# A layer of attention and routed experts: setup for the first batch alone, the rest dealt over two units, and filler products counted per step

## The reference

```python
xn = layernorm(x)
q, k, v = split(xn @ w_qkv)                       # 16 heads of 8
wei = softmax(where(causal, q @ k.T * 8 ** -0.5, -inf))
attn = (wei @ v) @ w_proj + b_proj
top2, idx = top_k(xn @ Wg.T, 2);  w = softmax(top2)
y = sum over k of w[k] * (gelu(xn @ W1[idx[k]] + b1[idx[k]]) @ W2[idx[k]] + b2[idx[k]])
out = x + attn + y
```

## Time and profile before

| | us |
|---|---|
| median of 3 runs | 864.74 (863.75 to 866.88) |
| profiled execution | 862.67 |
| its span, first to last instruction | 860.9 |
| PE busy, share of span | 737.2 (86%) |
| DVE busy | 557.6 (65%) |
| ACT busy | 449.3 (52%) |
| POOL busy | 282.8 (33%) |
| mean granted clock of TensorE | 0.849 |

### The profile page before, as it was taken

One profiled execution on the slowest core, in us unless ns is written; L12 is line 12 of the kernel. 1 busy time (PEld: TensorE's weight loads), 2 busy tenths in 40 slices (PEclk: granted clock), 3 DMA queues, 4 the chain that ended last, 5 costly groups with the idle time before them and its releaser, 6 DMA issues.

```text
span 860.9 us, 15136 instructions
## 1 busy us (share of the span) xinstructions
PE 737.2 (86%) x5021; PEld 418.5 (49%) x5021; DVE 557.6 (65%) x2164; ACT 449.3 (52%) x717; POOL 282.8 (33%) x454
## 2 busy tenths in 40 slices
PE   3683788988888989879999999889999999999995
PEld 2562344434445545545555455546455555546543
DVE  5649455556575676757676766757767667676656
ACT  2212133243445666656655665646666665566663
POOL 7103835657121323323231313122332223131421
PEclk9555566559786999999898989889999989897998
DMA  6997301203074342606134342505242423430074
GB/s 156 174 148 247 133 25 35 77 32 79 18 221 137 83 124 58 173 13 166 59 92 113 87 120 81 151 13 146 80 126 87 120 84 88 137 109 4 22 180 124
DMA packets 96261, 88.74 MB, mean 103 GB/s; under 512 B 8368, under 2 KB 83672, under 8 KB 96184
## 3 DMA queue, kind: packets, MB, share of 16 engines
q1 hardware_dynamic: 91432, 78.05, 35.2%
q0 software_dynamic: 4544, 9.35, 3.3%
q10 hardware_dynamic: 208, 0.38, 0.2%
...
## 4 chain that ended last, share of the span: by engine, by line
PE 66%; DVE 18%; SPq 4%; DMA 3%; issue 3%; ACT 3%; POOL 2%; another core or an unknown queue 0%; ACTq 0%; DVEq 0%
PE ov L780 19%; PE aux L748 16%; PE aux L838 10%; PE aux L790 6%; DVE maxes L970 5%; DVE junk L971 3%; SPq L449 3%; PE sc L702 3%; PE aux L795 3%; DMA hid<-in_L_ffn_W 2%; PE sc L703 2%; PE sc L704 2%; DVE maxes L966 2%; DVE xrow L1024 2%; PE aux L818 1%
## 5 line engine op out<-in xcount | busy, mean ns | idle before, releaser
L655 ACT ACTIVATE probs<-sc 128x1024 f32<-128x1024 f32 (+3 forms) x384 | 295.1, 810 | 252.6 <-PE sc L766 235.0
L748 PE MATMUL aux<-kT,qT 32*128 32x512 f32 (+3 forms) x768 | 244.3, 484 | 67.4 <-DVE maxes L971 19.5
L568 POOL TENSOR_SCALAR_AFFINE_SELECT probs<-probs 128x256 f32<-128x256 f32 x256 | 103.9, 409 | 390.3 <-ACT probs L655 386.0
L970 DVE TENSOR_REDUCE maxes<-aux 128x1 f32<-128x128 f32 (+2 forms) x384 | 161.1, 420 | 66.5 <-PE aux L748 65.5
L966 DVE TENSOR_REDUCE maxes<-aux 128x1 f32<-128x512 f32 x256 | 163.4, 684 | 60.9 <-PE aux L748 52.4
L748 PEld LDWEIGHTS aux<-kT,qT 32*128 32x128 f32 x768 | 108.2, 205 | 181.7 <-DVE maxes L971 50.4
L780 PE MATMUL ov<-probs,v 128*32 128x512 f32 (+3 forms) x1536 | 186.8, 562 | 3.6 <-POOL probs L568 3.4
L766 PE MATMUL sc<-qT,kT 32*128 32x512 f32 (+3 forms) x768 | 170.8, 466 | 5.5 <-DMA qT<-mT 5.1
L971 DVE CUSTOM_DVE_ANT_0 junk<-aux,cst 128x128 f32<-128x128 f32 x512 | 140.6, 283 | 17.5 <-PE aux L748 16.3
L593 POOL DMA_INDIRECT ys<-ysb,back x78 | 76.0, 974 | 77.4 <-issue 46.2
L838 PEld LDWEIGHTS aux<-w2b,hid 128*128 128x128 f32 x624 | 78.7, 197 | 41.8 <-DVE maxes L971 28.8
...
## 6 DMA issues: line engine op xcount, KB each, us to landing
...
```

The lines of the kernel that those rows point to most:

```text
L568: nc.gpsimd.affine_select(out=block_, in_=block_, compare_op=ALU.is_ge, fill=0.0, base=0, pattern=[[0, 2], [1, P]], channel_multiplier=-1) ...
L655: nc.scalar.activation(probs[:, s % 2, 2 * half:2 * half + 2, 0:cols], pair(part)[:, :, 0:cols], ACT.Exp).then_inc(sc_done, 1)
L748: nc.tensor.matmul(bank(part)[:, 0:cols], qT[n % 3][rows, P * i:P * i + P], kT[n % 3][rows, k0:k0 + cols], start=True, stop=True).then_inc ...
L970: nc.vector.reduce_max(maxes[:, i, other, h:h + 1], bank(part)[:, 0:cols - P], axis=AX.X)
```

## The change

The setup handles batch 0 alone. Stats and norm of batches 1 and 2 are started in it, with the norm of batches 1 to 3 now on GpSimd; all three vg groups of batch 0 stand in it (the groups are regrouped by batch, 12 in all); 24 maxima instead of 16 come ahead of unit 0, with 20 fillers before them and three before each pair. The table `BESIDE` deals the rest over the steps of unit 0 (xt, vg, stats and norm of batch 3, the split of W1 in two parts, cast and store, and the clearing in 13 pieces) and of unit 1 (the routing in 12 pieces, `route`, of one to six instructions each). The routing's scratch moves from `probs` to the space of `w2b`, `attnT` and `xsin`, and the first exponential no longer waits for the routing. Relay 0 is issued by SP and ScalarE, three transfers each. W1 is loaded by eight transfers. The transfers that zero the fourth rows of the queries fall away for the first three units, which a memset has zeroed.

The 64 scatters go to 22 steps, from step 10 of unit 1 to step 7 of unit 3. The experts' blocks are dealt over units 4 to 14, eleven instead of twelve, three or four a unit (five units with three, six with four). The stream of maxima is dealt anew: a unit takes its own last 16 in its first steps (24 in units 0 and 2) and then the next unit's first 32 (24 in unit 1); the last unit, which had none, has 16. `rows` comes one step after its `negate`. Loading for the first expert group starts in step 8 instead of 7.

A filler is now a product of 128 x 128 x 384 of type f32r, in one record instead of two per product. `fill` counts how many a step gets: each part's columns, times passes, times its share of the array, are summed from the step's start to the next step or to the next hidden product, and what lacks to 4000 (units 0 to 3), 2900 (expert units) or 3300 (unit 15) is filled up. Applied to the list this gives 339 products: 56 in the setup, 23, 37, 50 and 44 in units 0 to 3, 8 or 9 in each of units 4 to 13 (six in step 0, none in step 1, up to one in step 9, two in step 11), 14 in unit 14 and 30 in unit 15. In units 0 to 3 a full step has one to four, steps with short values up to eight.

```diff
+FILL = 384
...
+EARLY_M = 24
+
+FFN_UNIT = list(range(4, UNITS - 1))
 GROUP_OF = {u: f for f, u in enumerate(FFN_UNIT)}
 NGRP = len(FFN_UNIT)
 FIRST = [NBLK * f // NGRP for f in range(NGRP + 1)]
-VG_TILES = [list(range(t, min(t + 3, NT))) for t in range(0, NT, 3)]
+VG_TILES = [[TPB * b + t for t in x] for b in range(B) for x in ((0, 1, 2), (3, 4, 5), (6, 7))]
+PIECES = 13
...
-    parts = [("weights",), ("stats", 0), ("stats", 1), ("norm", 0), ("xt", 0), ("xt", 1)]
+    parts = [("weights",), ("stats", 0), ("norm", 0), ("xt", 0), ("xt", 1)]
     parts += [("qk", 0, j, c) for c in range(2) for j in range(2)]
-    parts += [("relay", n) for n in range(2)] + [("clear",), ("fetch",), ("relay", 2)]
-    parts += [("norm", 1), ("xt", 2), ("stats", 2), ("xt", 3), ("vg", 0), ("norm", 2), ("stats", 3), ("xt", 4), ("vg", 1),
-              ("xt", 5), ("vg", 2), ("norm", 3), ("xt", 6), ("vg", 3), ("xt", 7)]
-    maxima = [("max", 0, m) for m in range(HALF_M)]
-    for r in range(4, len(VG_TILES)):
-        parts += maxima[2 * r - 8:2 * r - 6] + [("vg", r)]
-    parts += [("top_two",)] + maxima[14:] + [("negate", 0, 0), ("prefix",), ("rows", 0, 0), ("slots",)]
-    parts += [("w1", e) for e in range(E)] + [("scatter", t, 0) for t in range(4)]
+    parts += [("fetch", e) for e in range(E)] + [("relay", 0), ("relay", 1)]
+    parts += [("vg", 0), ("stats", 1), ("norm", 1), ("vg", 1), ("vg", 2), ("stats", 2), ("norm", 2)]
+    parts.append(("warm", -1, 0, 20))
+    for i in range(0, EARLY_M, 2):
+        parts += [("warm", -1, i + 1, 3)] + with_negations(maxima()[i:i + 2])
+        if i + 2 == HALF_M:
+            parts.append(("rows", 0, 0))
     return parts
+BESIDE = {
+    (0, 0): [("relay", 2), ("w1", 0), ("clear", 0), ("clear", 1)],
+    (0, 1): [("xt", 2), ("w1", 1), ("clear", 2)],
+    (0, 2): [("xt", 3), ("w1", 2), ("w1_out", 0), ("clear", 3)],
+    (0, 3): [("vg", 3), ("w1", 3), ("w1_out", 1), ("clear", 4)],
+    (0, 4): [("vg", 4), ("stats", 3), ("norm", 3), ("w1_out", 2), ("clear", 5)],
+    (0, 5): [("vg", 5), ("xt", 4), ("w1_out", 3), ("clear", 6)],
+    (0, 6): [("xt", 5), ("vg", 6), ("clear", 7)],
+    (0, 7): [("vg", 7), ("w1", 4), ("clear", 8)],
+    (0, 8): [("vg", 8), ("xt", 6), ("w1", 5), ("clear", 9)],
+    (0, 9): [("xt", 7), ("vg", 9), ("w1", 6), ("w1_out", 4), ("clear", 10)],
+    (0, 10): [("vg", 10), ("w1", 7), ("w1_out", 5), ("clear", 11)],
+    (0, 11): [("vg", 11), ("w1_out", 6), ("clear", 12)],
+    (1, 0): [("route", 0), ("w1_out", 7)],
+    (1, 1): [("route", 1), ("route", 2)],
+    (1, 2): [("route", 3)],
+    (1, 3): [("route", 4), ("gate",), ("prefix",)],
+    (1, 4): [("route", 5)],
+    (1, 5): [("route", 6)],
+    (1, 6): [("route", 7)],
+    (1, 7): [("route", 8)],
+    (1, 8): [("route", 9), ("route", 10)],
+    (1, 9): [("route", 11)],
+}
...
-def unit_parts(n):
+def counts(n):
+    if n in GROUP_OF:
+        return [3] * NS
+    first = {0: [8, 8, 8], 1: [6, 5, 5], 2: [8, 8, 8]}.get(n, [6, 5, 5])
+    rest = {0: 32, 1: 24, UNITS - 1: 0}.get(n, 32)
+    return first + [rest * (i + 1) // 9 - rest * i // 9 for i in range(9)]
+def unit_parts(n, stream):
...
-    full_array = ("rows_in", "turn", "columns", "project", "qk", "down", "hidden")
     step_of = (2, 3, 4, 5, 7, 8) if len(subs) == 6 else range(2, 2 + len(subs))
-    here = 0
     for s in range(NS):
-        count = -(-len(todo) // (NS - s))
-        if n == 0:
-            count = 8 if s < 4 else 6
-        group = take(count)
-        if not any(x[0] in full_array for x in parts[here:]):
-            parts.append(("warm", n, s))
-        here = len(parts)
-        parts.extend(row_phase(n, s, group[:4]))
-        parts.extend(group[4:] + after_maxima(group))
+        due, late_rows[:] = list(late_rows), []
+        group = take(counts(n)[s])
+        parts.append(("step", n, s))
+        only = [x for x in group if x[0] == "max"]
+        parts.extend(row_phase(n, s, only[:4]))
+        parts.extend(x for x in group if x not in only[:4])
         if s == 0 and f is None:
             late_values()
         if s > 0:
             parts.append(("values", n, s - 1))
-        if s == 0 and n > 0:
-            parts.append(("rows", n, 1))
-        if s == 3 and n == 0:
-            parts.append(("rows", 0, 1))
-        if s == 7 and n + 1 < UNITS:
-            parts.append(("rows", n + 1, 0))
+        parts.extend(due)
+        parts.extend(BESIDE.get((n, s), []))
...
-        if n < 2:
-            i = 4 + 30 * n + (5 * s + 1) // 2
-            for x in range(i, 4 + 30 * n + (5 * s + 6) // 2):
-                parts.append(("scatter", x, 0))
+        step = NS * n + s - (NS + 10)
+        if 0 <= step < 22:
+            parts.extend([("scatter", 0, 0)] * (TOPK * NT * (step + 1) // 22 - TOPK * NT * step // 22))
...
+def aim(n):
+    return 2900 if n in GROUP_OF else 3300 if n == UNITS - 1 else 4000
+def array_use(part):
+    what = part[0]
+    if what == "scores":
+        return SUB[part[2]][3] // 2
+    if what == "values":
+        return 4 * SUB[part[2]][3]
+    if what == "max":
+        return MAXES[part[2] // HG][2] // 4
+    return {"turn": 1024, "xt": 1024, "columns": 1024, "rows_in": 1024, "project": 2048, "down": 2048, "rows": 256,
+            "qk": 3 * W, "vg": 9 * (C + E), "hidden": 12 * BK}.get(what, 0)
+def fill(parts):
+    out = []
+    for i, x in enumerate(parts):
+        if x[0] != "step":
+            out.append(x)
+            continue
+        end = next((j for j in range(i + 1, len(parts)) if parts[j][0] == "step" or parts[j][0] == "hidden"), len(parts))
+        n, s = x[1:]
+        short = aim(n) - sum(array_use(y) for y in parts[i:end])
+        if short > 0:
+            out.append(("warm", n, s, -(-short // FILL)))
+    return out
...
-        tmp = probs[:, :, :, :].rearrange("p a b w -> p (a b w)")
+        tmp = w2all[:, :, :, :].rearrange("p a b c -> p (a b c)")
+        scan = [attnT[:, 416 * i:416 * i + 416].rearrange("p (t e) -> p t e", e=E) for i in range(2)]
+        tmp2 = xsin[:, :, :].rearrange("p t c -> p (t c)")
...
+                        if n == 0:
+                            continue
                         sp.dma_start(qT[i][r:P:4, :].bitcast(F32), (kqh, kqh, kql)[r][rows, 1, :].bitcast(F32)) \
                             .then_inc(relayed[i], 16)
-                    sp.dma_start(qT[i][3:P:4, :].bitcast(F32), mid(zero[0:32, :], T // P)).then_inc(relayed[i], 16)
+                    if n >= 3:
+                        sp.dma_start(qT[i][3:P:4, :].bitcast(F32), mid(zero[0:32, :], T // P)).then_inc(relayed[i], 16)
                 elif what == "fetch":
-                    sp.dma_start(w1_in, W1.rearrange("e h i -> h e i")).then_inc(w1_loaded, 16)
+                    e = part[1]
+                    sp.dma_start(w1_in[:, e, :], W1[e]).then_inc(w1_loaded, 16)
                 elif what == "clear":
+                    i = part[1]
                     sp.wait_ge(dest_set, 2)
-                    tiles = xs.rearrange("(g v p) c -> v p g c", p=P, v=SPARE)
-                    for i in range(SPARE):
-                        sp.dma_start(tiles[i], mid(zrow[:, i, :], SLOTS // P // SPARE)).then_inc(xs_zero, 16)
+                    sp.dma_start(xs.rearrange("(g v p) c -> g p v c", p=P, v=SPARE)[i], zrow).then_inc(xs_zero, 16)
                 elif what == "rows":
                     n, c = part[1:]
                     sp.wait_ge(aux_a, A_AFTER[part])
                     sp.dma_start(qT[n % 3][3:P:4, W * c:W * c + W].bitcast(F32), mT[:, :].bitcast(F32)) \
                         .then_inc(rows_set[c], 16)
-                elif what == "w1":
+                elif what == "w1_out":
...
-                    if i == 1:
+                    if i == 0:
...
+                elif what == "norm" and part[1] > 0:
+                    i = part[1]
+                    pool.wait_ge(rstd_ready, i + 1)
+                    for t in range(TPB * i, TPB * i + TPB):
+                        last_ = nc.gpsimd.tensor_scalar(xn[:, t, :], xn[:, t, :], meanvar[:, t, 0:1], rstd[:, t:t + 1],
+                                                        ALU.subtract, ALU.mult)
+                        if t % 4 == 3:
+                            last_.then_inc(xn_ready, 1)
...
+                if part == ("relay", 0):
+                    act.wait_ge(zeroed, 9)
+                    act.wait_ge(aux_d, D_AFTER["qk", 0, 1, 1])
+                    for r in range(3):
+                        act.dma_start(qT[0][r:P:4, :].bitcast(F32), (kqh, kqh, kql)[r][0:32, 1, :].bitcast(F32)) \
+                            .then_inc(relayed[0], 16)
...
-                    if (n, s) == (0, 0):
-                        act.wait_ge(slots_ready, 1)
...
-                        for _ in range(WARM):
-                            nc.tensor.matmul(bank(unit)[:, 0:P], ident, upper, start=True, stop=True)
+                        for _ in range(part[3]):
```

(8 more changed lines are left out.)

146 lines of the change are left out of this document (71 added, 75 removed).

## The result

The changed kernel takes 856.1 us (median of 19 runs, 848.9 to 863.7) against 863.3 for the kernel before in the same comparison (19 runs): ratio 0.991, 95% interval 0.989 to 0.993. So the change is a gain of 7 us, not of 75. The profiled execution took 850.3 us with a span of 848.6.

What follows compares the result with a forecast made beforehand. It took the start as bound by a chain, later stretches by TensorE, busy 84 to 91% and slower at low clock. Start and units 0 to 3 243.5 + expert units 502 + last 40 = 786 us span, 3.8 over it: 790; range 766 to 830.

Steps and rivals of the forecast that it cites:

- First exponential 41.5: Start: first maximum at 27.5, maxima 9.5, negation to exponential 4.5, so first exponential at 41.5 us; bounds 38 and 50.
- Unit 0, 51: Unit 0: three steps of 5.5, nine at 3.4 and smaller terms make 51 us, before 76.8; bounds 45 and 65.
- unit 1, 50: Unit 1: VectorE's maxima, low halves, turns and routing sum to 44, with waits 50 us; bounds 44 and 56.
- Units 2 and 3, 101: Units 2 and 3: GpSimd's scatter steps 84, four more steps 13.6, late loads 3, making 101 us; bounds 94 and 120.
- 3.4 would be TensorE's pace: Scatter steps of units 2 and 3: TensorE alone would need 3.4 us a step, less than GpSimd's 4.35 or 3.7.
- Eleven expert units 502: Units 4 to 14: 517 less 25 saved by fillers, plus 4.5 for blocks and 5.5 for maxima; bounds 490 and 517.
- Last unit 40: Unit 15: 39 us before, +4 for 16 maxima coming in, -3 for shorter fillers, making 40 us.
- (1): Rival, 13%: the low clock stays in units 0 to 3, 24 steps take 5 us; time 831 us.
- (2): Rival, 15%: maxima wait for the relay behind W1's loads, or unit 4 for its loads; 12 to 15 us, time 804.
- (3): Rival, 9%: expert units' step 0 fillers come on the path and the clock falls all the same; time 826 us.
- (4): Rival, 3%: f32r fillers do not hold TensorE's clock, expert units run at 1.2 GHz; time some 1000 us.
- The rule on GpSimd: Unit 1's routing: two-input VectorE instructions share ports with GpSimd and meet only selects; some 3 us, inside the unit's bounds.

Runs made afterwards that it cites:

- experiment 1: Changed kernel with GpSimd's memsets of qT, mneg and v waiting for VectorE's normalisation of the first batch; ratio 0.979 to the kernel before.
- experiment 14: Kernel of experiment 9 with 16 instead of 24 maxima in the setup, the rest dealt to unit 0's first three steps; ratio 0.971 to the kernel before.
- Experiment 15: Kernel of experiment 9 with at least six fillers in steps 1 and 2 of units 0 to 3; ratio 0.974 to the kernel before.
- experiment 9: Kernel of experiment 1 with 16 maxima moved from unit 15 to units 2 and 3, last row transposed in the next unit's step 0; ratio 0.966 to the kernel before.
- experiment 10: Kernel of experiment 1 with the 64 scatters dealt over the same 22 steps by step length; ratio 0.974 to the kernel before.
- experiment 2: Changed kernel with the 64 scatters replaced by plain SyncE transfers of the same bytes, output wrong; ratio 0.977 to the kernel before.
- experiment 6: Changed kernel without the six fillers in step 0 of the eleven expert units; ratio 1.006 to the kernel before.
- 7: Kernel of experiment 1 with fewer fillers in the start and none in step 0 of unit 0; ratio 0.981 to the kernel before.
- 11: Kernel of experiment 1 with the six fillers of each expert unit's step 0 moved to that step's end; ratio 0.979 to the kernel before.
- 12: Kernel of experiment 1 with scatters dealt by step length and expert units' step 0 fillers moved to that step's end; ratio 0.971 to the kernel before.
- experiment 13: Kernel of experiment 9 with the scatters dealt by the length of the step; ratio 0.965 to the kernel before.

## Why the prediction was wrong

It had the mechanisms mostly right and called the sign, but all six terms of the sum were too low. Errors of one sign don't cancel, and the range was made as if they did.

- **"First exponential 41.5"**, 57.6 measured. The start's old chain is gone as forecast. Two parts failed. The memsets moved with the first batch were not among the moved instructions that I costed; experiment 1 prices them at 7 us. And "from the negation to the exponential that needs it takes 4.4 us" forgot the eight further maxima and their fillers, which the list puts between the two; experiment 14 prices them at 7.6. The rest, some 1 to 2 us, lies ahead of the first maximum, which came at 28.75 in experiment 1 where 27.5 was forecast.
- **Unit 0, 51; unit 1, 50**: 55.6 and 53.1. "5.5 a step" for the first three was the term: steps 1 and 2 of unit 0 take 7.7 and 8.7. I took VectorE's part as the step's length. (The norm on GpSimd was also mis-sized, 0.78 us a piece where 0.35 were assumed, but no select waited for it.) The trace of the changed kernel shows the two engines in turn, in step 1 of unit 2:

```profile
170.85 2.48 DVE L1060 TENSOR_REDUCE maxes<-aux 128x1 f32<-128x512 f32 x4 [0.50 <-issue]
171.60 3.01 PE L836 MATMUL aux<-kT,qT 32*128 32x512 f32 x5 [0.40 <-issue]
174.54 1.94 PE L868 MATMUL ov<-probs,v 128*32 128x512 f32 x8
176.41 1.12 PE L883 MATMUL aux<-cst,ot 128*128 128x128 f32 x4
177.17 1.63 PE L878 MATMUL aux<-wh 128*128 128x384 f32 x4
```

  With three banks TensorE can't run ahead of VectorE by more than three maxima, so values, turn and fillers come behind the maxima, at 1.2 GHz, while VectorE has nothing (it idles 2.06 us there before its next reciprocal). Experiment 15 shows that feeding TensorE more doesn't shorten these steps, though the clock over the first three steps is higher than in 9 in three of the four units. That the order of the parts would, or more banks, is argued and not tested.
- **Units 2 and 3, 101**: 112.2. GpSimd as the new bound was right, and its sum too: 84 us were forecast for the twenty scatter steps of units 2 and 3, by the same prices 92 for all 22, and 92.0 is what it takes where it is hardly ever idle (experiment 10). What failed is the other engine's price and with it the overlap: "3.4 would be TensorE's pace", and without scatters these 22 steps take 85 us, not 75 (experiment 2: 6.8 in unit 1, 48.7 in unit 2 and 29.6 in unit 3). Of two sums so near each other the larger is not the length, because the deal is even and the steps are not: in those of 2 us three scatters are late, in those of 8.7 they leave GpSimd idle (11.6 us in the changed kernel), and what is late at step 7 of unit 3 makes the steps behind it late (step 8 takes 8.4 us instead of the 4.9 of experiment 2). The loss against experiment 2 is 17 us in units 2 and 3, part of it through the low clock after a wait; but 2 to 6 us of it belong to this one execution, since the four traces with the same list there (experiments 1, 6, 7 and 11) take 106.6 to 109.9. The new deal brings the two units down to 101.6 (experiments 10 and 12), so it accounts for about half of the loss.
- **"Eleven expert units 502"**: 521. The saving was right: steps 0 to 2 take 8.74 us on average instead of 10.96, 2.2 a unit against the 2.3 forecast, though the clock still fell in four units. So was the price of the longer maxima between the blocks: from the first hidden product of unit 7 to its first scores it takes 9.81 us without fillers (experiment 6) and took 9.23 before, 0.6 against 0.5. Wrong was that the six fillers stand "where TensorE waits for VectorE anyway": they stand behind such a wait, and the same stretch of unit 7 takes 10.96 us with them and 9.81 without: 1.15 us a unit, 13 in all. Unit 4 pays 5.9 more than unit 7 in its hidden phase, at the low clock, after TensorE waited 3.95 us for the first blocks' W1 (3 were forecast, in the stage before); in experiment 1, where that wait is 1.2, it pays 1.9. Their loads stand on SP behind the packed rows (issued at 265.92) and x:

```profile
266.34 4.82 SPq L539 DMA_DIRECT2D xrow<-in_L_attn_x  x4
272.26 2.78 SPq L559 DMA_DIRECT2D w1b<-w_scr  x3
277.90 0.55 PE L790 MATMUL sc<-xsh,w1b 128*128 128x256 f32 x1 [3.95 <-issue]
278.25 0.41 PE L791 MATMUL sc<-xsl,w1b 128*128 128x256 f32 x1
```

- **"Last unit 40"**: 49.6. The term "+4" for 16 maxima should have been 8 or more (experiment 9 takes 8.4 away with them).
- **The rivals.** (1), the low clock, has its first half: unit 1 ran at 0.71 and units 2 and 3 at 0.79, the clock of before. (2), the slip of the start, has the second half, for other reasons than W1's loads. (3) is right in that the fillers come on the path and wrong in that they buy nothing. (4) is out: f32r fillers hold the clock.
- **The rule on GpSimd.** I applied the Trainium skill's page SBUF — State Buffer, section SBUF: two separate sides, to the routing alone. It says that VectorE and GpSimd share a pair of ports, which the one that starts first holds for its whole instruction while the other stands still. The first normalisation shows just that, and more: its first two pieces, of 0.27 us each otherwise, begin at 12.70 and 12.96, behind the start of the first memset (12.55), and end behind the last, so they stood still through five memsets (three of qT, one of mneg, one of v) and not through one. The condition that the GpSimd instruction reads SBUF, which I took into my words, the page sets only for a VectorE instruction with two inputs there; it names one in a mode that uses both ports beside it, without the condition. So page and row don't differ, and I had used half of the rule. Whether this tensor_scalar runs in such a mode no trace shows.

Of what the change gained in the start and unit 0 (49 us on the scores of unit 1) the traces show 36 given back behind it: 3 in unit 1, 19 in units 2 and 3, 5 in the expert units and 10 in the last. Mending three faults (memsets, maxima, scatters; experiment 13) gives 0.965, 30 us under the kernel before and 22 under the change; memsets and maxima alone give 0.966 (experiment 9).
